# Six experts of a routed feed-forward layer: slots moved instead of held in the second layer, block transposes on VectorE, output written in quarter rows

## What is computed

```
x = layernorm(h)                                   # 592 x 256
logits = (x @ w_red) @ normalised(wg).T            # 592 x 8
idx, score = argmax and maximum of softmax(logits)
hid = gelu(x @ w1[idx] + b1[idx])                  # 1024 wide
out = h + (hid @ w2[idx] + b2[idx]) * score
```

## Time and profile before

| | us |
|---|---|
| median of 3 runs | 129.36 (128.86 to 130.53) |
| the profiled execution | 130.33 |
| its span, first to last instruction | 128.4 |
| TensorE busy | 120.5 (94%) |
| VectorE, ScalarE, GpSimd busy | 56.7, 48.1, 42.7 |
| DMA: 19,681 packets, 32.75 MB | mean 255 GB/s |

### The profile page before, as it was taken

The page is one execution under the profiler, slowest core; times in us unless marked ns, Lnnn a source line. Parts: engine busy times, 40 slices in busy tenths (PEclk is TensorE's granted clock), DMA queues, the critical chain, the costliest instruction groups (busy, mean ns, idle before and its releaser), DMA issues.

```text
span 128.4 us, 3559 instructions
## 1 busy us (share of the span) xinstructions
PE 120.5 (94%) x1460; PEld 102.0 (79%) x1460; DVE 56.7 (44%) x178; ACT 48.1 (37%) x145; POOL 42.7 (33%) x58
## 2 busy tenths in 40 slices
PE   7969999999999999999999899999999999999970
PEld 2747887877667878798799798899898999999850
DVE  1140599661996858798987300160212121220210
ACT  0300002447486666666456760036333150606000
POOL 8800014590059039272857800032020202011022
PEclk9999999999999999999999999999999999999999
DMA  4899999137919999999999947999999999200011
GB/s 114 289 334 385 390 405 394 67 125 174 171 36 205 149 269 360 390 365 379 365 402 369 362 141 212 321 298 343 381 378 384 362 388 333 68 5 25 3 29 31
DMA packets 19681, 32.75 MB, mean 255 GB/s; under 512 B 1779, under 2 KB 13686, under 8 KB 19662
## 3 DMA queue, kind: packets, MB, share of 16 engines
q1 hardware_dynamic: 18126, 30.06, 72.2%
q0 software_dynamic: 768, 2.12, 4.6%
q10 hardware_dynamic: 768, 0.31, 0.9%
HBM read 27.41 MB, written 5.38 MB: 255 GB/s over the span
## 4 chain that ended last, share of the span: by engine, by line
PE 68%; DMA 15%; issue 8%; POOL 3%; SPq 2%; ACT 1%; DVE 1%; POOLq 0%
PE ps L818 18%; PE ps L834 16%; PE ps L543 9%; DMA w2s<-v_scratch 6%; DMA early<-embed_in 5%; DMA v_scratch<-hz 4%; PE ps L734 4%; PE ps L602 4%; PE ps L690 3%; PE ps L703 3%; PE ps L609 3%; PE ps L799 2%; POOL vbd L1186 2%; PE ps L672 2%; POOL out L1233 1%
## 5 line engine op out<-in xcount | busy, mean ns | idle before, releaser
L834 PE MATMUL ps<-w2s,early 128*64 128x256 f32 (+1 forms) x256 | 29.2, 379 | 0.0
L525 ACT ACTIVATE early<-ps,b1s 128x112 f32<-128x112 f32 x64 | 17.4, 354 | 30.4 <-PE ps L818 30.4
L818 PE MATMUL ps<-early,w1s 128*64 128x112 f32 x512 | 26.1, 259 | 0.5 <-issue 0.5
L818 PEld LDWEIGHTS ps<-early,w1s 128*64 128x64 f32 x512 | 25.6, 137 | 1.0 <-issue 0.8
L834 PEld LDWEIGHTS ps<-w2s,early 128*64 128x64 f32 (+1 forms) x256 | 23.1, 130 | 3.4
L543 PE MATMUL ps<-early 128*128 128x256 f32 x60 | 15.0, 403 | 1.3 <-DMA early<-embed_in 1.2
L543 PEld LDWEIGHTS ps<-early 128*128 128x128 f32 x60 | 11.6, 200 | 4.1 <-DMA early<-embed_in 2.6
L1106 DVE COPY early<-ps 128x224 f32<-128x224 f32 x6 | 2.4, 392 | 24.4 <-PE ps L799 24.4
L1233 POOL DMA_INDIRECT out<-pos,early x4 | 3.8, 943 | 24.7 <-DVE pos L1124 24.4
L1233 POOL DMA_INDIRECT out<-pos,wide x4 | 3.8, 942 | 20.0 <-DVE pos L1124 20.0
L609 PE MATMUL ps<-xnt,wqkv 128*128 128x296 f32 x32 | 9.1, 422 | 0.0
(11 more groups left out here) (141 smaller groups left out, 172.7 us busy)
## 6 DMA issues: line engine op xcount, KB each, us to landing
w1s<-w SPq DMA_DIRECT2D x8, 1024.0 KB, 9.9
w2s<-w SPq DMA_DIRECT2D x8, 1024.0 KB, 12.7
early<-embed_in SPq DMA_DIRECT2D x5, 448.0 KB, 7.8
slot_scratch<-nil SPq DMA_DIRECT2D x1, 2240.0 KB, 14.6
early<-slot_scratch SPq DMA_DIRECT2D x4, 280.0 KB, 4.1
wide<-slot_scratch SPq DMA_DIRECT2D x4, 280.0 KB, 6.3
b2s<-b SPq DMA_DIRECT2D x4, 256.0 KB, 7.8
wqkv<-w_qkv SPq DMA_DIRECT2D x1, 768.0 KB, 11.0
```

Of the source, the lines that this page charges most:

```text
L525: nc.scalar.activation(gt[:, t % 2, f, :], ps[:, 2 * (t % 2) + f // 4, (f % 4) * CAP:(f % 4 + 1) * CAP], ACT.Gelu, bias=b1t[:, f:f + 1]).t ...
L818: m = nc.tensor.matmul(ps[a * ROW_B:(a + 1) * ROW_B, 2 * (t % 2) + f // 4, (f % 4) * CAP:(f % 4 + 1) * CAP], w1s[:, r, k, c:c + ROW_B], xt ...
L834: m = nc.tensor.matmul(ps[n0:n1, 4 + t % 2, 0:D], gt[:, t % 2, f, n0:n1], w2s[:, r, f, :], start=(f == 0), stop=(f == FT - 1))
```

## The change

- A row in the scratch tensor now begins with 128 numbers of head (score and token number last), then the own values, then the normalised ones (`AHEAD`).
- Slots are numbered so that slot 4a+i takes column 32i+a after turning (`QB`, `NQ`, `CA`); 128 slots per expert are cleared and loaded, of which 112 are used.
- The normalised half of experts 2 to 7 is loaded in quarters (`load_blocks`): partition 32b + a gets quarter b (64 numbers) of slots 4a to 4a+3. VectorE turns it by transposes of 32 x 32 blocks straight into `xt` (`rows_turned`); TensorE's turnings go. w1 of these experts is loaded with feature 2p+k on partition p.
- For experts 0 to 5 (`TURNED`) and in the overflow path the second layer holds w2, whose columns the host has put in another order, and moves the slots. The result has features on partitions; ScalarE adds the bias (`result_turned`), VectorE turns it back by block transposes and adds, in four quarters (`result_blocks`), and GpSimd writes each expert with four scatters of quarter rows. Their own values are loaded in quarters too, with score and number four times, one for each quarter (`load_rows`).
- Experts 6 and 7 keep the second layer as it was (`result_rows`), with their rows in one load each.
- SP issues after the spreading: quarters of 2 and 3, rows of 0 to 3, weights of 4, quarters and rows of 4 and 5, weights of 5, quarters and rows of 6 and 7, weights of 6 and of 7.
- The second bias is loaded once as columns for all experts and as rows for two; the two products of `bout` stand a little later.

```diff
+QB = 32
+NQ = P // QB
+CA = CAP // NQ
-ROW = 2 * D + 128
+AHEAD = 128
+ROW = AHEAD + 2 * D
+TURNED = 6
...
+        def turned_out(t):
+            return t < TURNED or t >= E
+        def meta_of(t):
+            return buffer_of(t)[:, 0:2 * NQ].rearrange("p (i m) -> p i m", m=2)
+        def blocks_of(t):
+            return buffer_of(t)[:, AHEAD + D:ROW]
+        def slots_of(t, k):
+            if t < ONCHIP:
+                return xt[:, t, k, 0:CAP]
+            return xt[:, t % 2, k, :].rearrange("p (i a) -> p i a", i=NQ)[:, :, 0:CA]
...
-            sp.dma_start(of_expert[0:CAP, :, :], nil[0:CAP, :].unsqueeze(1).to_broadcast([CAP, E, ROW]))\
+            sp.dma_start(of_expert[0:P, :, :], nil[:, :].unsqueeze(1).to_broadcast([P, E, ROW]))\
...
-            for e in range(0, E, 2):
-                sp.dma_start(b2s[:, e:e + 2, :], b2[e:e + 2].partition_broadcast(P)).then_inc(q["loaded_b2"], 16)
+            sp.dma_start(b2c[:, :, :], b2_c).then_inc(q["loaded_b2c"], 16)
+            sp.dma_start(b2s[:, :, :], b2[TURNED:E].partition_broadcast(P)).then_inc(q["loaded_b2"], 16)
...
-            def load_rows(t):
-                sp.dma_start(row_of(t), of_expert[0:CAP, t, :]).then_inc(gathered[t], 16)
+            def load_blocks(t, slots):
+                sp.dma_start(blocks_of(t).rearrange("p (i n) -> p i n", i=NQ),
+                             slots[:, AHEAD + D:ROW].rearrange("s (b n) -> b s n", b=NQ)).then_inc(blocks_in[t % E], 16)
+
+            def load_rows(t, slots):
+                cols = slice(AHEAD - 2, AHEAD + D)
+                if turned_out(t):
+                    sp.dma_start(buffer_of(t)[:, AHEAD:AHEAD + D].rearrange("p (i n) -> p i n", i=NQ),
+                                 slots[:, AHEAD:AHEAD + D].rearrange("s (b n) -> b s n", b=NQ)).then_inc(gathered[t % E], 16)
+                    sp.dma_start(meta_of(t), slots[:, AHEAD - 2:AHEAD].unsqueeze(0).to_broadcast([NQ, P, 2]))\
+                      .then_inc(gathered[t % E], 16)
+                else:
+                    sp.dma_start(row_of(t)[:, cols], slots[0:CAP, cols].rearrange("(a i) n -> i a n", i=NQ))\
+                      .then_inc(gathered[t % E], 16)
 
             sp.wait_ge(q["spread"], 16 * NT)
-            for t in (*range(ONCHIP, RING), *range(ONCHIP), *range(RING, E)):
-                load_rows(t)
+            for t in range(ONCHIP, RING):
+                load_blocks(t, of_expert[0:P, t, :])
+            for t in range(RING):
+                load_rows(t, of_expert[0:P, t, :])
             for t in range(RING, E):
                 load_expert(t)
+                if t < RING + 2:
+                    for a in (2 * t - RING, 2 * t - RING + 1):
+                        load_blocks(a, of_expert[0:P, a, :])
+                        load_rows(a, of_expert[0:P, a, :])
...
+            def result_turned(t):
+                act.wait_ge(q["yt_cleared"], 1)
+                act.wait_ge(q["y_ps"], t + 1)
+                if t >= 2:
+                    act.wait_ge(q["yb_ready"], t - 1 if t < E else t - 1 - (E - TURNED))
+                for k in range(KD):
+                    m = nc.scalar.activation(yt[:, t % 2, k, :].rearrange("p (i a) -> p i a", i=NQ)[:, :, 0:CA],
+                                             ps[:, 4 + 2 * (t % 2) + k, 0:CAP].rearrange("p (i a) -> p i a", i=NQ),
+                                             ACT.Identity, bias=tile_of(t)[2][:, k:k + 1])
+                m.then_inc(q["yt_ready"], 1)
...
+                    if turned_out(t):
+                        for k in range(KD):
+                            for a in range(2):
+                                c = k * P + a * ROW_B
+                                m = nc.tensor.matmul(ps[a * ROW_B:(a + 1) * ROW_B, 4 + 2 * (t % 2) + k, 0:CAP],
+                                                     w2s[:, r, f, c:c + ROW_B], gt[:, t % 2, f, :],
+                                                     start=(f == 0), stop=(f == FT - 1))
+                        continue
...
             def rows_turned(t):
-                dve.wait_ge(q["xt_ps"], t - ONCHIP + 1)
+                dve.wait_ge(blocks_in[t % E], 16 if t < E + ONCHIP else 32)
                 dve.wait_ge(q["hidden_ps"], 2 * (t - 1))
-                V.tensor_copy(xt[:, t % 2, :, :],
-                              ps[:, 6 + t % 2, 0:KD * CAP].rearrange("p (k n) -> p k n", k=KD))\
-                    .then_inc(q["xt_ready"], 1)
+                V.transpose(xt[:, t % 2, :, :].rearrange("p k (i a) -> p k i a", i=NQ),
+                            blocks_of(t).rearrange("p (i c k) -> p k i c", i=NQ, c=QB)).then_inc(q["xt_ready"], 1)
+
+            def result_blocks(t):
+                n = t if t < E else t - (E - TURNED)
+                dve.wait_ge(gathered[t % E], 32 * (t // E + 1) if t % E < TURNED else 16 * (t // E + 1))
+                V.tensor_scalar(ids_of(t), meta_of(t).bitcast(U32)[:, :, 1], float(NQ), C("quarter"), ALU.mult, ALU.add)\
+                    .then_inc(q["id4_ready"], 1)
+                dve.wait_ge(q["yt_ready"], n + 1)
+                if t >= 2:
+                    dve.wait_ge(scattered[t % 2], scatters(t))
+                V.transpose(yb[:, t % 2, :].rearrange("p (i k c) -> p k i c", i=NQ, k=KD),
+                            yt[:, t % 2, :, :].rearrange("p k (i a) -> p k i a", i=NQ)).then_inc(q["yb_ready"], 1)
+                dve.wait_ge(q["yb_ready"], n + 1)
+                for i in range(NQ):
+                    of = slice(i * ROW_B, (i + 1) * ROW_B)
+                    m = V.scalar_tensor_tensor(yout[:, t % 2, of], yb[:, t % 2, of], meta_of(t)[:, i, 0:1],
+                                               buffer_of(t)[:, AHEAD:AHEAD + D][:, of], ALU.mult, ALU.add)
+                m.then_inc(q["y_ready"], 1)
...
+                if turned_out(t):
+                    for i in range(NQ):
+                        pool.indirect_dma_start(out_quarters, bass.IndirectOffsetOnAxis(ids_of(t)[:, i:i + 1], 0),
+                                                yout[:, t % 2, i * ROW_B:(i + 1) * ROW_B], None,
+                                                bounds_check=last_quarter, oob_is_err=False).then_inc(scattered[t % 2], 16)
+                    return
...
```

More of the change, by code:

```diff
@@ L108, in constants @@
     put("pow", np.array([[-0.5, 0.5]]))
+    put("quarter", p[:, None] // QB + 2 * NOROW * NQ * (p[:, None] % QB >= CA))
     put("patch", (tok < T) & (tok % S > 0))
@@ L250, in vit_tower, with buffer_of, ids_of, scatters @@
         gt = late(2 * FT * CAP).rearrange("p (b f n) -> p b f n", b=2, f=FT)
-        xt = late(2 * KD * CAP).rearrange("p (b k n) -> p b k n", b=2, k=KD)
+        xt = late(2 * KD * P).rearrange("p (b k n) -> p b k n", b=2, k=KD)
         yout = pos[:, 0:2, :]
-        hsum = sb("hsum", [P, 2, D])
+        hsum = sb("hsum", [P, E - TURNED, D])
+        def buffer_of(t):
+            r = t % E
+            return rows[:, r, :] if r < RING else more[:, r - RING, :]
         def row_of(t):
-            r = t % E
-            return rows[0:CAP, r, :] if r < RING else more[0:CAP, r - RING, :]
+            return buffer_of(t)[0:CAP, :]
+        def turned_out(t):
+            return t < TURNED or t >= E
+        def meta_of(t):
+            return buffer_of(t)[:, 0:2 * NQ].rearrange("p (i m) -> p i m", m=2)
+        def ids_of(t):
+            return buffer_of(t)[:, 2 * NQ:3 * NQ].bitcast(U32)
+        def scatters(t):
+            n = [(NQ if turned_out(u) else 1) for u in range(t % 2, t, 2)]
+            return 16 * sum(n)
+        def blocks_of(t):
+            return buffer_of(t)[:, AHEAD + D:ROW]
         w1s = sb("w1s", [P, RING, KD, F])
@@ L304, in vit_tower @@
         gathered = [sem(f"gathered{t}") for t in range(E)]
+        blocks_in = [sem(f"blocks_in{t}") for t in range(E)]
         block = ctx.enter_context(nc.Block())
@@ L869, in _ @@
             V = nc.vector
[L871 removed]
+            V.memset(nil[:, AHEAD:ROW], 0.0)
             dve.wait_ge(q["loaded_cf"], 16)
@@ new lines, in result_rows @@
+            def result_rows(t):
+                score = row_of(t)[:, AHEAD - 2:AHEAD - 1]
+                dve.wait_ge(gathered[t], 16)
+                V.scalar_tensor_tensor(hsum[0:CAP, t - TURNED, :], b2s[0:CAP, t - TURNED, :], score, row_of(t)[:, AHEAD:AHEAD + D],
+                                       ALU.mult, ALU.add).then_inc(q["hsum_ready"], 1)
+                dve.wait_ge(q["hsum_ready"], t - TURNED + 1)
+                dve.wait_ge(q["y_ps"], t + 1)
+                dve.wait_ge(scattered[t % 2], scatters(t))
+                V.scalar_tensor_tensor(yout[0:CAP, t % 2, :], ps[0:CAP, 4 + 2 * (t % 2), 0:D], score,
+                                       hsum[0:CAP, t - TURNED, :], ALU.mult, ALU.add).then_inc(q["y_ready"], 1)
@@ L1258, in _ @@
                         scatter(E + i)
-                        pool.wait_ge(scattered[i % 2], 16 * ((E + i) // 2 + 1))
+                        pool.wait_ge(scattered[i % 2], scatters(E + i + 2))
 _OUT = ((B, S, D), "float32")
```

131 lines of the change are left out of this document (62 added, 69 removed).

## The result

The changed kernel takes **153.01 us** (median of four runs, 152.36 to 155.08) against 129.38 for the kernel before beside it: ratio 1.177, 95% interval 1.170 to 1.183. The forecast was 151 us, slower. The profiled execution took 152.61 us, span 150.8 (before 130.33 and 128.4).

What follows compares the result with a forecast made beforehand. TensorE was taken as the bound, DMA engines 2.5 us behind. To 130.33 us, +19.1 for TensorE's later end and +2.2 for scatter pieces gave 151.6, or 151 us beside the median; range 124.5 to 166.

Steps and rivals of the forecast that it cites:

- TensorE's own saving: Experts 0 to 5: second layer 3.07 us instead of 3.46, six turnings gone; -4.7 us in sum.
- Small work on the other engines: Expert stage: ScalarE's 0.7 us, VectorE's at most 3.7 and GpSimd's 3.8 per expert stay hidden.
- Four engines: New loads, four outermost at the source, are shared by 4 DMA engines, not 16; chance 0.68.
- Rival (b): New loads spread over all 16 DMA engines, nothing is late, TensorE's saving comes out whole: 125 us; chance 0.22.
- The price of a piece: DMA pieces of the new loads: 17.3 ns for 256 bytes, 5.9 ns for 8 bytes.
- (a): Four DMA engines and dear pieces of 35 ns: +27 us, 178 us; chance 0.15, within the 0.68 for four engines.
- (c): All 16 DMA engines but pieces at 35 ns: 130.5 us, no change a measurement can tell; chance 0.07.
- The busiest engines' queue: Loads of experts 2 to 7 queue on four DMA engines; TensorE ends at 143.5 instead of 124.4 us, +19.1.
- The clock: Granted clock, whole kernel: stays at 1.00, the upper of two levels, so no price depends on it.
- The scatter's pieces: Quarter scatters' pieces, 32 on each DMA engine per expert, add 4 x 0.55 = 2.2 us.
- The end of the chain: From TensorE's last product to the end: stays 4.0 us, as the last two experts keep one scatter.
- Rival (d): Result writes of 256 bytes are read-modify-write; scatter pieces' 2.2 us doubled, 153 us; no chance of its own given.

Runs made afterwards that it cites:

- e3: Kernel before, with only the row loads of experts 2 to 7 naming slots as 4 outermost at the source: 143.73 us, ratio 1.108.
- e7: Kernel before, with the row loads of experts 2 to 7 naming slots as 8 outermost at the source: 134.5 us, ratio 0.999.
- e12: Changed kernel, quarter loads with 128 slots outermost on both sides (16 engines each), values mixed up: 135.91 us, ratio 1.043 to the kernel before.
- e10: Kernel before with VectorE turning token rows, second layer and scatter unchanged, blocks in four cut loads in needed order: 138.00 us, ratio 1.043.

## Why the prediction was right, point by point

In short: the mechanism was right and is shown. The closeness of the number, 1.0 us, is in part luck: three errors of 0.8 to 2.6 us offset each other, and two of some 1.5 us do so earlier on; both places are named below.

**TensorE's own saving: right.** L899 takes 3.07 us per expert (expert 5: 132.74 to 135.81) and the turnings are gone. The runs of 28 slots cost nothing: 259 ns per product, as a first layer at full clock. Second layers began at 74.13 us instead of 75.78; that 1.6 us is not in the sum, and 0.5 of it is a stop of the kind above in the trace of before.

**Small work on the other engines: right.** A block transpose took 442 ns, at the lower end of my bounds, an Identity pass 355, a quarter's addition 282. None stands ahead of TensorE except where its load was late.

**Four engines: right, and shown.** The new loads on q1 end on 4 completions each: 25,694 packets less 24,912 pieces that the code asks for leave 782 = 42 x 16 + 6 x 5 + 20 x 4. The Trainium skill's rule (DMA: Bandwidth & Descriptors, "Why a DMA increments its semaphore by 16 and not by 1"), the largest count up to 16 that divides the outermost index of both sides, held for loads whose two sides differ: here with 4 completions a load, in e3 with 4 (72 packets fewer than before) and in e7 with 8 (48 fewer). Rival (b) falls with the queue rows and with e12: undoing this alone for the twelve quarter loads gave back 17 of 23.6 us.

**The price of a piece: right for quarters, too low for numbers.** Issue times of 1.8 to 2.15 us for 512 quarters stand beside my 2.2, and the trace's packet records have 18 ns for 256 bytes beside my 17.3. Loads of numbers took 1.24 us and more beside 0.75 (8-byte packets 9 ns, not 5.9), some 1.6 us more for the four ahead of expert 4's weights. What hid that was luck: the loads were released at 75.34 us, 1.5 sooner than the 76.88 of the sum. So expert 4's first weights landed at 91.27 + 6.6 = 97.9, where the sum had them (95.2 and half of 5.6: 98.0; its 100.8 is for both layers' weights), and so did its blocks, issued behind them. Rivals (a) and (c), 35 ns, fall.

**The busiest engines' queue: right.** Expert 4's rows at 103 (measured: first layer from 103.3), expert 5's first weights (111.1 + 2.8 = 113.9 by the sum's steps, 114.65 landed: 107.95 + 6.7), expert 6's first layer at 127.4 (127.11), expert 7's weights at 132.5 (121.90 + 11.6 = 133.5). TensorE's end, 143.5 in the sum, came at 145.9.

**Wrong in size, three terms that nearly cancel.** The clock: I took 1.00 throughout. After its waits TensorE ran three first layers at 5.56, 4.78 and 5.63 us instead of 3.07, 6.8 us in all, of which only the last, 2.6, is on the path, because the other two are followed by a wait for weights that absorbs them. The scatter's pieces: I added 2.2 us, and nothing shows them. Weights landed when the queue without them says, and the packets of q0, which carries the scatters, took no more time in all than before: 4.0% of 16 x 150.8 us against 4.6% of 16 x 128.4, 97 and 95 us of one engine; my 2.2 us on each of sixteen would be 35 more.

```profile
q0 software_dynamic: 1248, 2.13, 4.0%
```

before:

```profile
q0 software_dynamic: 768, 2.12, 4.6%
```

The end of the chain: I left it at 4.0 us, and it grew to 4.9. I had said that a last expert would feel four scatters, but the scatters of expert 5 did not hold up expert 7's. That one waited for VectorE and began 0.86 us after TensorE's last product, as before:

```profile
146.81 0.95 POOL L1324 DMA_INDIRECT out<-pos,wide  x1 [2.42 <-DVE pos L1202]
```

before:

```profile
125.21 0.94 POOL L1233 DMA_INDIRECT out<-pos,wide  x1 [2.51 <-DVE pos L1124]
```

What grew stands behind it: GpSimd's drain, the instruction with which it closes the program, took 3.04 us instead of 2.27. In all ten traces with quarter scatters it took 3.02 to 3.10, in the four without (before, e3, e7, e10) 2.21 to 2.32. So the longer drain goes with the quarter scatters; why is open. In all, 143.5 + 2.2 + 4.0 + 1.9 = 151.6 was forecast and 145.9 + 4.9 + 1.8 = 152.6 measured.

**Rival (d)** is not borne out: 4 scatters of 256-byte pieces took q0 no more packet time than one of 1 KB pieces did, 97 against 95 us in all. As these records don't tell reads from writes, a cost that they leave out is not excluded, but none of the forecast's 2.2 us is left for it.

**Where rival (b)'s 125 was too low.** Even with sixteen engines TensorE ends at 129.25 (e12). Without any wait it would end at 118.1, from its 86.42 us on; the 11.1 us between are the 4.9, 2.5 and 3.4 above, and 0.3 that these leave. Why expert 4's blocks need 8.3 us to land is open: the number loads still have four outermost, and two weight loads and 512 quarters are issued just ahead and behind, but no run changed these alone.

## What to carry to other kernels

Before adding a strided or broadcast load, look at the outermost index of both sides, not at its bytes: with 4 there, six row loads of unchanged bytes cost 13.7 us; with 8, nothing that the time could tell. Cutting such a load in parts moved the bound to the issuing queue (some 0.7 us each here), so swap the indices instead where the layout allows (e12 shows what that is worth, with values mixed up; a layout that keeps them was not tried). And where a change lightens the bound engine by a few us, price what it puts on the one next to it, with the second price of some of its waits, a slower clock behind them (first layers of 4.78 to 5.63 us behind the waits of after; in e10 they kept 3.29 behind waits of 1.60 to 2.35 us).

## What was unexpected of the hardware

- A load on four engines holds the issuing queue: mostly 1.8 to 2.15 us for an issue that took 0.51 to 1.36 on sixteen engines (e12), up to 6.46 with weights ahead. Everything behind it in that queue is late, though the DMA share from 79 to 91 us is 0.30.
- A cut load, 32 partitions by 4 pieces of 256 bytes, costs SP 0.60 us to issue (median; up to 1.06), some 0.7 us from one to the next, with the DMA share at 0.22, against 0.43 to 0.47 for 1 MB of weights.
- The same kernel took 135.9 and 145.6 us on two chips on which the kernel before took 129.6 and 133.0: TensorE stops that no wait explains, up to 1.0 us each.
- With quarter scatters GpSimd's closing drain took 3.02 to 3.10 us, without them 2.21 to 2.32, though the last scatter began equally soon behind TensorE's last product (0.85 to 0.88 us) in every trace.
